# Two changes of order in a two-layer graph network: the second normalisation of a graph stage, and the alternation of bends and gate in the output network

## The chip, the cores and the metric

The kernel runs on one core of a Trainium2 chip. The metric is the device time in microseconds (us) from start to end of one execution. The engines of the core are TensorE (PE, matrix products), VectorE (DVE), ScalarE (ACT, one function per element), GpSimd (POOL) and SyncE (SP, which issues transfers). They run side by side, each in the order of its own program, and wait for each other on semaphores. SBUF is the on-chip memory, PSUM the memory that TensorE writes.

## What is computed

The input x holds 64 graphs of 256 nodes with 256 numbers each; adj holds 64 adjacency matrices of 256 x 256. Four steps follow one another, each on a layer-normalised x and each added to x. The last two are the ones that the change touches:

```python
x = x + _L0_gnn_ref(_layernorm(x), adj, ...)        # gated graph convolution
x = x + _L0_ffn_ref(_layernorm(x), ...)             # an LSTM over the nodes, prefix and suffix sums
x = x + _L1_gnn_ref(_layernorm(x), adj, W, b)       # normalised adjacency times x W, plus b
x = x + _L1_ffn_ref(_layernorm(x), ...)             # the output network, below

t = jnp.max(xx[:, None, :] + Wt[None, :, :], axis=-1) + bt
cvx = jnp.max(z * sl_cvx[None] + of_cvx[None], axis=-1)      # z = t, 8 pieces
ccv = jnp.min(z * sl_ccv[None] + of_ccv[None], axis=-1)
trop = s * cvx + (1.0 - s) * ccv
classical = jax.nn.gelu(xf @ Wc + bc, approximate=False)
g = jax.nn.sigmoid(xf @ Wg + bg)
out = (g * trop + (1.0 - g) * classical) @ Wd + bd
```

## The kernel before

The program is a row of stages with everything in float32: the first graph stage, the LSTM, the second graph stage (`stage_gnn1`), a short stage that turns the 8 + 8 pieces of each of the 1024 hidden units into a base line and a list of hinges, the tropical maximum t (written to DRAM), and the output network (`stage_ffn`).

**The second graph stage** works in rounds of about 10.3 us. In round r five graphs are in work at different lags: `live(0)` is graph r (logits of the LSTM stage and the weighted rows `whf`, `whb`), lag 2 is graph r-2 (x2, its first normalisation `xn`, its degrees), lag 3 is graph r-3 (projection, aggregation, x3 and its statistics), lag 4 is graph r-4 (turned and stored). VectorE's round, in the order of its program: x2 and its statistics (L1006 to L990), `x2b` = x2 + bias (L1011), `xn` (L995, waits for GpSimd's `rstd`), logits and `whf`/`whb` (L1020 to L1028), x3 (L1040, reads TensorE's aggregation), its statistics, two small degree instructions, `s` (L1059), and last the second normalisation `xn3` of the same graph of lag 3 (also L995, since both normalisations go through the helper `normalised`; waits for GpSimd's `rstd3`). A normalisation is two instructions of 128x256. GpSimd takes the variance to the power -0.5: for `rstd` (L817, L819), then adds the identity to the next adjacency (L824), for `rstd3` (L830, L832), then the degrees' power (L838 to L841, `dinv`). TensorE's aggregation (L956) waits for ScalarE's `hs`, and that for `dinv`; the transposes of `xn3` (`ps_xn3t`) and `xn` (`ps_t`), both L906, end TensorE's round. SyncE stores x3 and xn3 of lag 4, then loads `adjt` of lag 1, stores the turned xn3, and loads the next `adj` and `x1`. The rounds 0 to 7 and the last six are written out, the others run in a loop of two rounds.

**The output network** takes tokens in 16 blocks of 1024 and hidden units in 8 groups of 128 per block; one group of one block is called a unit here (u is the group, q = 8m + u the number of the unit in the whole stage, m the block). For a unit, TensorE multiplies x with Wc and Wg in halves of 512 tokens (`products(q, h)`, L2586, into `ps_c` and `ps_g`, one bank each), turns the unit's t into `ps_t` (`turn`, L2578, one buffer), and multiplies the finished unit with Wd (`output_part`, L2599). Its order is: products(q, 0), turn(q+1), products(q, 1), output_part(q-1). ScalarE makes from `ps_t` the base line (L2544) and one rectified hinge per knot: three sure ones (L2549), a number `more[u]` of further ones into the single buffer `spare` (L2556; 5, 2, 2, 1, 1, 1, 1, 1 for the groups 0 to 7), and a last sure one (L2558), which frees `ps_t`. Gelu (L2534, `cls`) and Tanh (L2536, `th`) of the halves lie between. VectorE adds each hinge times its bend onto the line (L2665, 128x1024, each bend depends on the one before), and for the unit before it runs the gate in three instructions, each dependent on the one before: line minus cls (L2645), times (th + 1) (L2648), times 0.5 plus cls into `fused` (L2652). In group 1 `total` (L2661, two instructions) closes the block before: it reads `ps_o`, and TensorE's first output product of a block waits for it.

Before, VectorE's unit is: three bends, (total), the three parts of the gate of the unit before, the fourth bend, the spare bends, and an instruction on one number (`pause`) after which `spare` may be written again.

## Time and profile before

| | us |
|---|---|
| median of 3 runs | 6393.19 (6391.79 to 6393.27) |
| the profiled execution, its own time | 6392.52 |
| its span from first to last instruction | 6390.7 |
| VectorE busy | 5095.3 (80%) |
| TensorE busy | 5520.0 (86%) |
| ScalarE busy | 3238.1 (51%) |
| GpSimd busy | 1914.4 (30%) |

The busy shares are means over stages with different limits, so they do not tell what an edit in one stage is worth. The second graph stage lies at about 1720 to 2390 us, the output network from 4807 us to the end; between them are stages that the change leaves alone. The time of a stage is read from the distance at which one of its instructions comes back, and its limit from the engine that does not wait in that distance. In the rows, "x3" is a run of three instructions, the second number is its length, and the brackets give idle time of the engine just before and what ended it. Instructions of one engine overlap by some hundredths of a microsecond, so a step is measured from start to start.

### The profile page before, as it was taken

How to read it: one execution, taken by the hardware profiler on the slowest of the kernel's cores; microseconds unless marked ns; L12 is line 12 of the kernel's file. 1: busy time of each engine (PE TensorE's matmuls, PEld its weight loads, DVE VectorE, ACT ScalarE, POOL GpSimd, SP SyncE). 2: the span in 40 equal slices, each digit the busy share in tenths (PEclk: the TensorE clock that was granted, in tenths of full speed). 3: DMA queues.
4: the chain of work that ended last, by engine and by line, in shares of the span. 5: the costliest groups of instructions: out<-in, count | busy, mean ns of one | idle time of the engine just before them, and what ended most of it. 6: DMA issues, size and time to landing. Idle time of an engine off the chain costs nothing. (4 is left out here: it accounts for less than half of the span.)

```text
span 6390.7 us, 100252 instructions
## 1 busy us (share of the span) xinstructions
PE 5520.0 (86%) x27318; PEld 3377.2 (53%) x27318; DVE 5095.3 (80%) x9609; ACT 3238.1 (51%) x6025; POOL 1914.4 (30%) x4567
## 2 busy tenths in 40 slices
PE   9998888888788871999999996676667999999999
PEld 6664555555577761666666664444433444444444
DVE  8995444444488877999999998897777999999998
ACT  6663222222244440666666663121116777777777
POOL 3331111111144441555665563147360000000000
PEclk9999999999999995999999998898888999999999
DMA  4441000000144442122212221147352221221221
GB/s 137 134 136 39 0 0 0 0 0 0 41 153 153 153 142 72 69 74 74 73 69 74 74 74 45 54 155 243 109 200 97 79 79 66 86 79 66 79 86 46
DMA packets 359563, 528.72 MB, mean 83 GB/s; under 512 B 28000, under 2 KB 298080, under 8 KB 359424
## 3 DMA queue, kind: packets, MB, share of 16 engines
q1 hardware_dynamic: 323120, 401.16, 19.2%
q0 software_dynamic: 36304, 126.13, 5.8%
q14 instruction: 103, 0.84, 0.0%
q8 instruction: 36, 0.59, 0.0%
HBM read 298.06 MB, written 229.13 MB: 82 GB/s over the span
## 5 line engine op out<-in xcount | busy, mean ns | idle before, releaser
L1743 PE MATMUL t_fetched<-t_wpart,t_onehot 128*128 128x512 f32 x4096 | 1222.3, 420 | 35.6 <-DVE t_tout L1848 15.5
L1848 DVE SCALAR_TENSOR_TENSOR t_tout<-t_fetched,t_top,t_tout 128x1024 f32<-128x1024 f32 x896 | 1149.1, 1282 | 36.4 <-PE t_fetched L1743 5.2
L1743 PEld LDWEIGHTS t_fetched<-t_wpart,t_onehot 128*128 128x128 f32 x4096 | 692.0, 188 | 271.6 <-DVE t_tout L1848 131.4
L2665 DVE SCALAR_TENSOR_TENSOR f_line<-f_hinge,f_vec,f_line 128x1024 f32<-128x1024 f32 x512 | 656.8, 1283 | 60.6 <-ACT f_hinge L2549 45.7
L2171 PE MATMUL ts_fetched<-t_wpart,ts_onehot 128*128 128x512 f32 x1608 | 506.8, 449 | 165.5 <-ACT ts_onehot L2146 66.4
L584 ACT ACTIVATE l_act<-l_ps 128x128 f32<-128x128 f32 x1024 | 228.2, 275 | 716.9 <-PE l_ps L601 716.9
L601 PE MATMUL l_ps<-l_whh,l_ht 128*64 128x256 f32 x4096 | 498.5, 385 | 103.2 <-DVE l_ht L571 103.2
L2599 PE MATMUL f_pso<-f_fused,f_wd 128*128 128x512 f32 x1024 | 464.8, 597 | 36.7 <-DVE f_fused L2652 36.7
L601 PE MATMUL l_ps<-l_wih,l_x 128*64 128x256 f32 x4096 | 485.6, 379 | 1.0 <-DVE l_ps L551 1.0
L2586 PE MATMUL f_psc<-f_x,f_wc 128*128 128x512 f32 x1024 | 485.6, 597 | 0.2
L2586 PE MATMUL f_psg<-f_x,f_wg 128*128 128x512 f32 x1024 | 481.8, 593 | 0.0
L2171 PEld LDWEIGHTS ts_fetched<-t_wpart,ts_onehot 128*128 128x128 f32 x1608 | 304.2, 207 | 316.6 <-DVE ts_tout L2239 209.2
L2143 ACT ACTIVATE ts_dist<-ts_index,t_pminus 128x256 f32<-128x256 f32 (+2 forms) x140 | 79.5, 568 | 656.3 <-PE ts_index L2162 626.1
L601 PEld LDWEIGHTS l_ps<-l_whh,l_ht 128*64 128x64 f32 x4096 | 271.7, 136 | 262.6 <-DVE l_ht L571 151.9
L2549 ACT ACTIVATE f_hinge<-f_pst,f_vec 128x1024 f32<-128x1024 f32 x384 | 398.8, 1114 | 0.0
L2239 DVE SCALAR_TENSOR_TENSOR ts_tout<-ts_fetched,ts_top,ts_tout 128x1024 f32<-128x1024 f32 x296 | 380.0, 1284 | 14.4 <-PE ts_fetched L2171 4.0
L518 POOL TENSOR_TENSOR l_pool_pause<-l_pool_zero 1x1 f32<-1x1 f32 x510 | 93.8, 184 | 972.0 <-DVE l_ht L571 956.1
L601 PEld LDWEIGHTS l_ps<-l_wih,l_x 128*64 128x64 f32 x4096 | 294.7, 137 | 148.9 <-issue 1.8
L2599 PEld LDWEIGHTS f_pso<-f_fused,f_wd 128*128 128x128 f32 x1024 | 192.5, 190 | 293.1 <-issue 266.3
L2556 ACT ACTIVATE f_spare<-f_pst,f_vec 128x1024 f32 x224 | 240.7, 1135 | 167.8 <-DVE f_pause L2690 167.6
L2586 PEld LDWEIGHTS f_psg<-f_x,f_wg 128*128 128x128 f32 x1024 | 195.2, 191 | 246.4 <-issue 246.4
L2665 DVE SCALAR_TENSOR_TENSOR f_line<-f_spare,f_vec,f_line 128x1024 f32<-128x1024 f32 x224 | 287.8, 1285 | 44.2 <-DVE f_line L2665 44.2
(389 smaller groups left out, 10719.4 us busy)
## 6 DMA issues: line engine op xcount, KB each, us to landing
t<-t_tout SPq DMA_DIRECT2D x128, 512.0 KB, 2.7
f_t<-t SPq DMA_DIRECT2D x64, 1024.0 KB, 5.3
g_adj<-in_adj SPq DMA_DIRECT2D x128, 256.0 KB, 3.0
g_adjt<-in_adjt SPq DMA_DIRECT2D x128, 256.0 KB, 2.7
t_x<-x_normalised SPq DMA_DIRECT2D x130, 128.0 KB, 2.4
g_x<-in_x SPq DMA_DIRECT2D x64, 256.0 KB, 2.7
x_kept<-g_x SPq DMA_DIRECT2D x64, 256.0 KB, 2.2
g_x<-x_kept SPq DMA_DIRECT2D x64, 256.0 KB, 2.8
```

Of the source, the lines that this page charges most:

```text
L518: pool.tensor_tensor(pool_pause[:, k:k + 1], pool_zero[:, :], pool_zero[:, :], ALU.add)
L584: act.activation(act_g[q][:, :], ps_g[r % 2][:, q // 2, (q % 2) * P:(q % 2 + 1) * P], ACT.Tanh if q == 0 else ACT.Sigmoid)\
L601: mm = pe.matmul(half(j, c2, p), source[:, k, :], w[:, k, 2 * p:2 * p + 2, c2, :], start=False, stop=last and k == KD - 1, skip_group_chec ...
L1743: mm = pe.matmul(fetched[c % RING][:, h * CH:(h + 1) * CH], one_hot[g][:, c % GRP * P:(c % GRP + 1) * P], w_part[part][:, k, h * CH:(h + 1 ...
L1848: dve.scalar_tensor_tensor(t_out[j][:, :], column[:, :], value, t_out[j][:, :], ALU.add, ALU.max)\
L2171: mm = pe.matmul(fetched[buf][:, h * CH:(h + 1) * CH], one_hot[b][:, at * P:(at + 1) * P], w_part[part][:, half, h * CH:(h + 1) * CH], sta ...
L2239: dve.scalar_tensor_tensor(t_out[j][:, :], column[:, :], top[j][:, c:c + 1], (t_out if c else t_in)[j][:, :], ALU.add, ALU.max).then_inc(f ...
L2549: op = act.activation(hinge[v][:, k, :], ps_t[:, :], ACT.Relu, bias=column(u, "knot", k))
L2556: act.activation(spare[:, ds(k, 1), :].rearrange("p o t -> p (o t)"), ps_t[:, :], ACT.Relu, bias=column(u, "knot", k + SURE))
L2586: mm = pe.matmul(ps_[:, :], w_[:, k, u * P:(u + 1) * P], x[j][:, k, h * HB:(h + 1) * HB], start=(k == 0), stop=(k == KD - 1))
L2599: mm = pe.matmul(ps_o[k][:, h * HB:(h + 1) * HB], w_d[:, u, k * P:(k + 1) * P], fused[u % 2][:, h * HB:(h + 1) * HB], start=(u == 0), stop ...
L2665: dve.scalar_tensor_tensor(acc[:, :], source, column(u, "bend", k), acc[:, :], ALU.mult, ALU.add)\
```

## The change

Two edits of order, neither of which adds or removes arithmetic.

In `stage_gnn1` VectorE's second normalisation moves from the end of the round (graph of lag 3) into the next round (then lag 4), behind `x2b` and ahead of the wait for `rstd`. In `stage_ffn` VectorE takes the gate apart into three pieces and runs one behind each of the first three bends, `total` comes behind them, and ScalarE signals each of the first three hinges by itself and puts Gelu and Tanh of the earlier unit's second half between them.

```diff
@@ stage_gnn1, vector @@
+                if live(4):
+                    n, i, j = graph(4)
+
+                    dve.wait_ge(rstd3_ready, n + 1)
+                    wait_past(dve, x3t_stored[j], 48 * i)
+                    normalised(n, xn3_out[j], x3, mv3, rstd3, xn3_ready)
+                if live(2):
+                    n, i, j = graph(2)
 
                     dve.wait_ge(rstd_ready, n + 1)
                     wait_past(dve, xt_done, n)
...
-                if live(3):
-                    n, i, j = graph(3)
-
-                    dve.wait_ge(rstd3_ready, n + 1)
-                    wait_past(dve, x3t_stored[j], 48 * i)
-                    normalised(n, xn3_out[j], x3, mv3, rstd3, xn3_ready)
@@ stage_ffn, scalar @@
+                    second_half = (lambda u_, q_, h_: None, classical, gate)
                     for k in range(SURE - 1):
-                        op = act.activation(hinge[v][:, k, :], ps_t[:, :], ACT.Relu, bias=column(u, "knot", k))
-                    op.then_inc(sure_ready, 1)
-                    if not (isinstance(q, int) and q == 0):
-                        gate((u - 1) % FT, q - 1, 1)
+                        if not (isinstance(q, int) and q == 0):
+                            second_half[k]((u - 1) % FT, q - 1, 1)
+                        act.activation(hinge[v][:, k, :], ps_t[:, :], ACT.Relu, bias=column(u, "knot", k))\
+                           .then_inc(sure_ready, 1)
...
@@ stage_ffn, vector @@
-                    dve.wait_ge(sure_ready, q + 1)
-                    for k in range(SURE - 1):
+                    for k, fuse_part in enumerate((fuse_diff, fuse_gate, fuse_sum)):
+                        dve.wait_ge(sure_ready, (SURE - 1) * q + k + 1)
                         if k > 0:
                             dve.wait_ge(chain, done + k)
                         bend(u, acc, hinge[v][:, k, :], k)
+                        if not (first and u == 0):
+                            fuse_part((u - 1) % FT, q - 1)
                     if u == 1 and not first:
                         total(m - 1)
-                    if not (first and u == 0):
-                        fuse((u - 1) % FT, q - 1)
```

VectorE at the seam of two rounds of the second graph stage, before (s1 ends the work on one graph, x2 begins the next round; xn30 is the second normalisation's buffer):

```order
L1059 TENSOR_TENSOR g1_s1<-g1_x11,g1_h2 128x512
L995 TENSOR_SCALAR g1_xn30<-g1_x3,g1_mv3,g1_rstd3 128x256 x2
...
L1006 TENSOR_TENSOR g1_x2<-g1_ps_y,g1_s0 128x512
...
L1011 TENSOR_TENSOR g1_x2b0<-g1_x2,g1_b 128x512
L995 TENSOR_SCALAR g1_xn<-g1_x2,g1_mv,g1_rstd 128x256 x2
```

and after:

```order
L1067 TENSOR_TENSOR g1_s1<-g1_x11,g1_h2 128x512
...
L1006 TENSOR_TENSOR g1_x2<-g1_ps_y,g1_s0 128x512
...
L1011 TENSOR_TENSOR g1_x2b0<-g1_x2,g1_b 128x512
L31 ISA
L995 TENSOR_SCALAR g1_xn30<-g1_x3,g1_mv3,g1_rstd3 128x256 x2
L995 TENSOR_SCALAR g1_xn<-g1_x2,g1_mv,g1_rstd 128x256 x2
```

The two instructions of xn30 stand now between x2b0 and xn, four steps later than before.

VectorE in one unit of the output network with one spare bend, before:

```order
L2665 SCALAR_TENSOR_TENSOR f_line3<-f_hinge1,f_vec,f_line3 128x1024
L2677 ISA
L2665 SCALAR_TENSOR_TENSOR f_line3<-f_hinge1,f_vec,f_line3 128x1024
L2677 REGISTER_ALU
L2665 SCALAR_TENSOR_TENSOR f_line3<-f_hinge1,f_vec,f_line3 128x1024
L2645 TENSOR_TENSOR f_line2<-f_line2,f_cls0 128x1024
L2648 SCALAR_TENSOR_TENSOR f_line2<-f_th0,f_line2 128x1024
L2652 SCALAR_TENSOR_TENSOR f_fused0<-f_line2,f_cls0 128x1024
```

and after:

```order
L2681 SCALAR_TENSOR_TENSOR f_line3<-f_hinge1,f_vec,f_line3 128x1024
L2653 TENSOR_TENSOR f_line2<-f_line2,f_cls0 128x1024
L2693 ISA
L2681 SCALAR_TENSOR_TENSOR f_line3<-f_hinge1,f_vec,f_line3 128x1024
L2660 SCALAR_TENSOR_TENSOR f_line2<-f_th0,f_line2 128x1024
L2693 REGISTER_ALU
L2681 SCALAR_TENSOR_TENSOR f_line3<-f_hinge1,f_vec,f_line3 128x1024
L2668 SCALAR_TENSOR_TENSOR f_fused0<-f_line2,f_cls0 128x1024
```

Bends onto line3 and gate parts on line2 alternate, with the same instructions and as many steps of the sequencer. ScalarE in the same place, before:

```order
L2544 ACTIVATE f_line3<-f_pst,f_vec 128x1024
L2549 ACTIVATE f_hinge1<-f_pst,f_vec 128x1024 x3
L2534 ACTIVATE f_cls0<-f_psc,f_vec 128x512
L2536 ACTIVATE f_th0<-f_psg,f_half_bg 128x512
```

and after:

```order
L2549 ACTIVATE f_line3<-f_pst,f_vec 128x1024
L2557 ACTIVATE f_hinge1<-f_pst,f_vec 128x1024
L2535 ACTIVATE f_cls0<-f_psc,f_vec 128x512
L2557 ACTIVATE f_hinge1<-f_pst,f_vec 128x1024
L2541 ACTIVATE f_th0<-f_psg,f_half_bg 128x512
L2557 ACTIVATE f_hinge1<-f_pst,f_vec 128x1024
```

The first hinge comes as before, the third two half-width instructions later.

## Rows read from the trace of the kernel before

**Rows 1.** Stages: length, then busy time (instructions) of PE, PEld, DVE, ACT, POOL; PEclk; DMA share; GB/s.

```profile
1760.00:2370.00 610.00, 545.03 (x3075) 463.99 (x3073) 502.50 (x1606) 287.68 (x647) 270.84 (x537) 1.00 0.49 152
4818.00:6391.00 1573.00, 1461.90 (x4124) 691.03 (x4122) 1440.34 (x1284) 1218.60 (x1381) 0.00 (x0) 0.99 0.22 75
```

**Rows 2.** Timeline of VectorE in one round of the second graph stage.

```profile
2061.59 0.74 DVE L995 TENSOR_SCALAR g_xn<-g_x,g_mv,g_rstd 128x256 f32<-128x256 f32 x2 [0.69 <-POOL g_rstd L832]
2062.24 0.69 DVE L1006 TENSOR_TENSOR g_x<-g_ps_y,g_s 128x512 f32<-128x512 f32 x1
...
2063.91 0.66 DVE L1011 TENSOR_TENSOR g_x2b<-g_x,g_b 128x512 f32<-128x512 f32 x1
2065.44 0.99 DVE L995 TENSOR_SCALAR g_xn<-g_x,g_mv,g_rstd 128x256 f32<-128x256 f32 x2 [0.86 <-POOL g_rstd L819]
...
2072.50 0.68 DVE L1006 TENSOR_TENSOR g_x<-g_ps_y,g_s 128x512 f32<-128x512 f32 x1
```

**Rows 3.** Timeline of GpSimd in the same round.

```profile
2060.30 1.16 POOL L832 TENSOR_TENSOR g_rstd<-g_vare,g_half 128x2 f32<-128x2 f32 x1
...
2064.07 0.56 POOL L817 TENSOR_TENSOR g_vare<-g_mv,g_eps 128x2 f32<-128x2 f32 x1 [1.43 <-DVE g_mv L990]
2064.71 0.69 POOL L819 TENSOR_TENSOR g_rstd<-g_vare,g_half 128x2 f32<-128x2 f32 x1
```

**Rows 4.** GpSimd's `keep`, all of its 64: nanoseconds shortest/median/longest.

```profile
L839 POOL TENSOR_TENSOR g_keep<-g_one,g_is_zero x64: 192/302/308, 1731.9 to 2376.6; 128x2 f32<-128x2 f32 x64
```

**Rows 5.** Timeline of TensorE, the two waits of the following round.

```profile
2073.84 1.99 PE L956 MATMUL g_ps_agg<-g_hs,g_adjt 128*128 128x256 f32 x8 [0.49 <-ACT g_hs L865]
2075.67 0.60 PE L906 MATMUL g_ps_xn3t<-g_ident,g_xn 128*128 128x128 f32 x4
2076.75 0.66 PE L906 MATMUL g_ps_t<-g_ident,g_xn 128*128 128x128 f32 x4 [0.48 <-DVE g_xn L995]
```

**Rows 6.** Output network, timeline of VectorE: unit 4 of a block, then units 0 and 1.

```profile
5463.32 3.92 DVE L2665 SCALAR_TENSOR_TENSOR f_line<-f_hinge,f_vec,f_line 128x1024 f32<-128x1024 f32 x3
5467.16 1.22 DVE L2645 TENSOR_TENSOR f_line<-f_line,f_cls 128x1024 f32<-128x1024 f32 x1
...
5469.67 1.23 DVE L2652 SCALAR_TENSOR_TENSOR f_fused<-f_line,f_cls 128x1024 f32<-128x1024 f32 x1
5470.81 1.28 DVE L2665 SCALAR_TENSOR_TENSOR f_line<-f_hinge,f_vec,f_line 128x1024 f32<-128x1024 f32 x1
...
5473.71 3.93 DVE L2665 SCALAR_TENSOR_TENSOR f_line<-f_hinge,f_vec,f_line 128x1024 f32<-128x1024 f32 x3
...
5506.46 3.93 DVE L2665 SCALAR_TENSOR_TENSOR f_line<-f_hinge,f_vec,f_line 128x1024 f32<-128x1024 f32 x3 [0.88 <-ACT f_hinge L2549]
...
5522.84 3.93 DVE L2665 SCALAR_TENSOR_TENSOR f_line<-f_hinge,f_vec,f_line 128x1024 f32<-128x1024 f32 x3
```

**Rows 7.** Timeline of ScalarE in unit 0: base line, the three hinges, last hinge.

```profile
5502.21 1.21 ACT L2544 ACTIVATE f_line<-f_pst,f_vec 128x1024 f32<-128x1024 f32 x1 [0.27 <-PE f_pst L2578]
5503.31 3.12 ACT L2549 ACTIVATE f_hinge<-f_pst,f_vec 128x1024 f32<-128x1024 f32 x3
...
5512.43 1.19 ACT L2558 ACTIVATE f_hinge<-f_pst,f_vec 128x1024 f32<-128x1024 f32 x1
```

**Rows 8.** Timeline of TensorE: one unit without a wait, unit 0's transposes, a slow output product.

```profile
5471.84 3.60 PE L2599 MATMUL f_pso<-f_fused,f_wd 128*128 128x512 f32 x8
5475.27 1.88 PE L2586 MATMUL f_psc<-f_x,f_wc 128*128 128x512 f32 x4
...
5483.01 3.60 PE L2599 MATMUL f_pso<-f_fused,f_wd 128*128 128x512 f32 x8
...
5501.05 1.04 PE L2578 MATMUL f_pst<-f_ident,f_t 128*128 128x128 f32 x8
...
5825.45 5.37 PE L2599 MATMUL f_pso<-f_fused,f_wd 128*128 128x512 f32 x8 [2.15 <-DVE f_fused L2652]
```

**Rows 9.** The chain that ended last: start, length, what; two turns' marks, first and last block.

```profile
4946.00 2.47 DVE f_ox L2661 x2
...
5460.56 3.70 PE f_pso L2599 x8
...
5556.61 3.70 PE f_pso L2599 x8
...
6301.30 2.47 DVE f_ox L2661 x2
```

More of the change, by code:

```diff
@@ L2528, in _, with classical @@
             more, _ = counts(act)
-            def gate(u, q, h):
+            def classical(u, q, h):
                 v, at = u % 2, slice(h * HB, (h + 1) * HB)
@@ L2534, in gate @@
                 act.activation(cls[v][:, at], ps_c[:, :], ACT.Gelu, bias=vec[:, u, 0:1]).then_inc(cls_ready, 1)
+            def gate(u, q, h):
+                v, at = u % 2, slice(h * HB, (h + 1) * HB)
                 act.wait_ge(g_done, 2 * q + h + 1)
@@ L2561, in body @@
                     wait_past(act, fused_ready, q - 1)
+                    classical(u, q, 0)
                     gate(u, q, 0)
             rounds(act, body)
+            classical(FT - 1, BLOCKS * FT - 1, 1)
             gate(FT - 1, BLOCKS * FT - 1, 1)
@@ L2638, in _, with fuse_diff @@
             more, before = counts(dve)
-            def fuse(u, q):
+            def fuse_diff(u, q):
                 v, acc = u % 2, line[u % 4]
@@ L2645, in fuse, with fuse_gate @@
                 dve.tensor_tensor(acc[:, :], acc[:, :], cls[v][:, :], ALU.subtract).then_inc(diff_ready, 1)
+            def fuse_gate(u, q):
+                v, acc = u % 2, line[u % 4]
                 dve.wait_ge(diff_ready, q + 1)
@@ L2648, in fuse, with fuse_sum @@
                 dve.scalar_tensor_tensor(acc[:, :], th[v][:, :], 1.0, acc[:, :], ALU.add, ALU.mult).then_inc(gated_ready, 1)
+            def fuse_sum(u, q):
+                v, acc = u % 2, line[u % 4]
                 dve.wait_ge(gated_ready, q + 1)
@@ L2692, in _ @@
             rounds(dve, body)
-            fuse(FT - 1, BLOCKS * FT - 1)
+            for fuse_part in (fuse_diff, fuse_gate, fuse_sum):
+                fuse_part(FT - 1, BLOCKS * FT - 1)
             total(BLOCKS - 1)
```

## The prediction, made before the change was run

> **What bounds the kernel now.** I read the stages' windows first [rows 1], then the timelines of each engine in one round or block, then the chain. The second graph stage is VectorE's: in 610 us it is busy for 502.5 and never waits for TensorE in a steady round. One round is 2072.50 - 2062.24 = 10.26 us (10.3 in the next; 10.28 is the mean I use), and in it VectorE stands still twice, both times for GpSimd: 0.69 us ahead of the second normalisation and 0.86 us ahead of the first [rows 2]. So 10.28 - 1.55 = 8.73 us is its own work. The transfers fill 0.49 of the DMA engines at 152 GB/s, and no engine waits for one. TensorE waits 0.49 and 0.48 us in a round [rows 5]; its own work is at most 10.28 - 0.97 = 9.3 us, and about 8.9 when the restarts behind these waits go as well (my estimate is some 0.2 us each).
>
> In the output network two engines are nearly equal. A unit takes TensorE 5483.01 - 5471.84 = 11.17 us when it does not wait [rows 8], so a block of 8 takes 89.4. VectorE needs 5473.71 - 5463.32 = 10.39 us for a unit with one spare bend; unit 0 with five spares takes 5522.84 - 5506.46 = 16.38 [rows 6]; a spare bend is (16.38 - 10.39) / 4 = 1.5, so unit 2 takes 11.9, and unit 1 with total's 2.4 takes 14.3; the sum is 16.4 + 14.3 + 11.9 + 5 x 10.39 = 94.5. The block comes back after 5556.61 - 5460.56 = 96.05 us, and over the 14 periods between first and last mark (6301.30 - 4946.00) / 14 = 96.8 [rows 9]. It is longer than either engine's work because the chain changes hands: VectorE sets the pace in the heavy units 0 to 2, TensorE in 3 to 7. The loop is: output product of unit 2 (5460.56), TensorE without a wait to the transposes of unit 0 (5501.05), ScalarE's line and three hinges (to 5506.43), VectorE without a wait to the gate of unit 2, next output product.
>
> **First edit: the second normalisation.** Removed is the wait of 0.69 us: when the next round comes to it, `rstd3` is over 2 us old. The pair itself takes 0.65 us (2062.24 - 2061.59) wherever it stands; now it stands in the gap between the end of x2b (2063.91 + 0.66 = 2064.57) and xn (2065.44), 0.87 us, of which it fills 0.65 and leaves 0.22 [rows 2]. Undisturbed, the round is 8.73 + 0.22 = 8.95 us. But GpSimd computes `rstd` in just that gap, and it is touchy there. Its power instruction takes 0.69 us alone and 1.16 when it meets VectorE's `s`; the small `vare` takes 0.56 under x2b [rows 3] and ends 0.06 us behind x2b; `keep`, which meets the second normalisation where that stands now, takes 302 ns in the median and 192 at the shortest [rows 4]. So a GpSimd instruction that starts under VectorE's reading waits until this is over. In the new place `rstd` would start at 2064.71, while xn3 runs from about 2064.50 to 2065.24. If it is held until 0.16 us before that end, as `keep` is, it starts at 2065.08, ends at 2065.77, and the round is 0.37 us longer: 9.3. If it is not held, 8.95. I take 9.15, the middle, somewhat to the `keep` row since that is the same pair of instructions. The ends that I keep are 8.73 (the wait vanishes) and 9.5 (held for the whole pair and `dinv` pushed under x2b too).
>
> The Trainium skill ("SBUF — State Buffer", Who interferes with whom) says that VectorE and GpSimd share one pair of ports, held as a lock: a VectorE instruction with two SBUF inputs, or in a two-port mode, blocks a GpSimd instruction that reads SBUF. The rows of `vare` and `rstd3` agree; whether a tensor_scalar of this form takes the pair is what [rows 4] suggest and the page ties to the mode. By the page at its hardest the round would be 9.4 to 9.5.
>
> TensorE's 8.9 to 9.3 lies just at the forecast: it doesn't undo the gain, but it would stop a round from going to 8.73. xn3's consumers have room: TensorE turns it behind the aggregation, which ended at 2075.67, 1.1 us after the new xn3 is done in its round's terms. Nothing else is queued behind the moved instructions on VectorE but xn, which comes at the same time as before. SyncE's wait for `xn3_ready` now holds the adjt load behind it, but that load already waits for the aggregation of the same round, which ends later; the load is used a round later. The wait for the stores of two graphs earlier gets a round more of slack. So: 60 steady rounds x (10.28 - 9.15) = **68 us**, with ends 60 x 0.8 = 48 and 60 x 1.4 = 84.
>
> **Second edit: alternating bends and gate.** VectorE first. From its first bend to the fourth is 5470.81 - 5463.32 = 7.49 us [rows 6]. Behind an instruction on which it depends, a bend comes at 1.32 us (3.92 for three is 2 x 1.32 + 1.28) and a gate part at 1.25; independent ones come at 5467.16 - 5463.32 - 2.64 = 1.20 behind a bend and at 5470.81 - 5469.67 = 1.14 behind a gate part. In the new order all six steps are independent of the one directly before: 3 x 1.20 + 3 x 1.14 = 7.02, 0.47 less. Four of the six steps existed as dependent ones. VectorE's block is then 94.5 - 8 x 0.47 = 90.7 us.
>
> The Trainium skill ("VectorE: DVE Perf Modes", The DRAIN you can't avoid) says the opposite: the next VectorE instruction waits for the pipe to empty anyway, and a semaphore between two costs nothing. The trace of this kernel disagrees by 0.1 us per step, and the rows decide. By the page the 0.47 would be zero.
>
> ScalarE: VectorE's first bend may start after one hinge, not three; that is 2 us earlier (3.12 for three, about 1.0 apart from start to start, [rows 7]). The second needs Gelu of the second half, whose products end 1.72 us behind the transposes while line and hinge keep ScalarE 2.1, so it does not wait; Tanh's products end at 3.45, ScalarE comes there at 3.7. The third hinge is 1.1 us later than before, 5.3 us behind the transposes' end, and VectorE asks for it 4.7 us after its own first bend, which is not before 2.1: covered. Relu, Gelu, Tanh and Identity already take turns: the 11.4 us from line to last hinge in unit 0 hold ten full-width and two half-width instructions at 1.0 and 0.6 us with no room for a change of tables, so the mixing costs nothing.
>
> Now the loops. The old one shrinks by 2.0 (one hinge) and four times 0.47 (VectorE passes through the first four steps of units 0, 1, 2 and 3): 96.05 - 3.9 = 92.2 us. Another becomes the longest, and this is where the gain stops. It goes through the end of unit 0. `total` now stands behind the gate in unit 1, and the block's first output product waits for it. From that product TensorE works without a wait through the transposes of the next unit 0: 6 x 11.17 less one half's products, 3.43 (5475.27 - 5471.84 is the same number of columns) = 63.6. ScalarE starts 1.16 us behind the transposes' start instead of 0.87 (5502.21 - 5501.05), adds 0.3, and needs 5512.43 + 1.19 - 5502.21 = 11.4 us for line, hinges, Gelu, Tanh, five spares and the last hinge, for which VectorE's fourth bend waits. VectorE then runs 16.38 - 7.49 = 8.9 to the end of unit 0, 7.0 to the end of the gate in unit 1, 2.5 for total. Handing over adds 0.2. Sum: 63.6 + 0.3 + 11.4 + 8.9 + 7.0 + 2.5 + 0.2 = 93.9. In unit 3 the transposes wait for ScalarE's spares of unit 2, up to 0.7 more; I take **94.3 us** a block. New waits: VectorE ahead of the fourth bend of unit 0 (some 2 us) and TensorE ahead of the first output product (some 2 us, now on `total`). Against the mean of 96.8: 15 blocks x 2.5 = **37 us**. Bounds: the loop of 92.2 gives 15 x 4.6 = 69; if the old loop keeps the pace for another reason, near 0. The page's rule would cost one 0.47 in this loop, 7 us of the 37.
>
> **Sum.** 68 + 37 = 105 us. The profiled execution took 6392.5 (span 6390.7 and 1.8 around it), the median is 6393.2: 6393.2 - 105 = **6288**.
>
> **The rivals.**
> The lock decides: `rstd` is held for the whole moved pair and the round goes to 9.45. For it: the `keep` row and the page. Then 60 x 0.83 = 50, and 50 + 37 = 87: 6306.
> The blocks do not shorten: TensorE's new wait for `total` and VectorE's for the last hinge of unit 0 eat what the first bend wins. For it: both waits are on the new loop and its sum is only 2.5 us under the old period. 68 + 5 = 73: 6320.
> The graph stage is held by something the timelines do not show, such as 152 GB/s of transfers [rows 1]; 1.57 MB a round in 9.15 us would be 171 GB/s. Against it: no engine in the round waits for a transfer, and VectorE's gaps end with GpSimd. Only the second edit pays: 6356, or nothing at all, 6393, if both fail.
> More than forecast: rounds at 8.8 and blocks at 92.5 give 60 x 1.45 + 15 x 4.3 = 152: 6241.
> Slower: TensorE's clock. Behind close waits one output product took 5.37 us instead of 3.60 [rows 8]: the granted clock had gone to half (1.2 of 2.4 GHz). A unit at half clock costs 11.2 us more. The new order gathers TensorE's waits around units 0 to 2 (about 4 us within 18). To end above 6393 it would have to eat 105 us: from 10 of the 128 units at half clock on; with 12 it is 6393 + 29 = 6422. Against it: the clock is 0.99 over the stage with 6.7 us of waiting a block, and 4.9 would be left.
>
> **How the numbers follow.** Forecast (both pay about as worked out, 6270 to 6300) 0.56; lock 0.14; blocks unchanged 0.11; more 0.08; graph stage held 0.04; nothing 0.03; slower 0.04. The range takes in the forecast, the lock and the blocks' rival, and the lower bounds of both costs in part: 6255 to 6325. 0.2% is 13 us, about what a measurement of this kernel tells from no change. Faster by more: 0.93; within: 0.03; slower: 0.04.
>
> **What would show it.** In the graph stage: the wait on `rstd3` gone, the one on `rstd` between 0.2 and 0.6, a round of 9.0 to 9.3, GpSimd's `rstd` (L819) over 691 ns. Shown wrong by a round over 9.5 or a wait of VectorE on TensorE. In the output network: 7.0 us from first to fourth bend, a wait ahead of the fourth bend in unit 0, TensorE waiting on `total`'s output, and 94.3 us from total to total. Wrong if TensorE waits more than 6 us a block, or the granted clock of the stage is under 0.97.

## The result, and the profile after

| | before | after |
|---|---|---|
| median of 4 runs each, us | 6392.49 | 6286.26 (6284.35 to 6286.68) |
| span of the profiled execution | 6390.7 | 6284.9 |
| VectorE busy | 5095.3 | 5046.8 |
| mean distance of `total` to `total`, 14 blocks | 96.81 | 95.29 |

The changed kernel takes 0.9834 of the time before, 95% interval 0.9816 to 0.9851, which is 106.2 us less; 6288 was predicted. The sum is nearer than its parts: the graph stage gave 83 us where 68 stood, the output network 23 to 26 where 37 stood.

**The graph stage.** VectorE in one round after the change (start, length, instruction, in brackets the idle time before it and its cause), to be held against [rows 2]:

```profile
2063.76 0.68 DVE L1006 TENSOR_TENSOR g_x<-g_ps_y,g_s 128x512 f32<-128x512 f32 x1
...
2065.43 0.66 DVE L1011 TENSOR_TENSOR g_x2b<-g_x,g_b 128x512 f32<-128x512 f32 x1
2066.01 0.73 DVE L995 TENSOR_SCALAR g_xn<-g_x,g_mv,g_rstd 128x256 f32<-128x256 f32 x2
2067.00 1.00 DVE L995 TENSOR_SCALAR g_xn<-g_x,g_mv,g_rstd 128x256 f32<-128x256 f32 x2 [0.25 <-POOL g_rstd L819]
...
2072.70 0.68 DVE L1006 TENSOR_TENSOR g_x<-g_ps_y,g_s 128x512 f32<-128x512 f32 x1
```

The round is 2072.70 - 2063.76 = 8.94 us; the next one is 8.88, and the steady rounds alternate between these two, 8.91 in the mean. The wait on `rstd3` is gone, the second normalisation stands in the gap, and 0.25 us of the gap of 0.87 is left. GpSimd in the same round, and all 64 of its `rstd` and `keep` (ns, shortest/median/longest), against [rows 3, 4]:

```profile
2066.22 0.74 POOL L819 TENSOR_TENSOR g_rstd<-g_vare,g_half 128x2 f32<-128x2 f32 x1
```

```profile
L819 POOL TENSOR_TENSOR g_rstd<-g_vare,g_half x64: 695/738/742, 1727.4 to 2288.2; 128x2 f32<-128x2 f32 x64
```

```profile
L839 POOL TENSOR_TENSOR g_keep<-g_one,g_is_zero x64: 187/190/206, 1732.5 to 2294.5; 128x2 f32<-128x2 f32 x64
```

`rstd` runs under the moved pair and takes 738 ns instead of 691: it was held up by 0.05 us, not by the 0.37 that I had feared. `keep` is back at 190 ns, since the pair has left it. From the first to the last of the 64 x2 instructions it is now 2285.7 - 1724.9 = 560.8 us; before it was 2368.1 - 1724.3 = 643.8. The difference is the 83 us. First after, then before:

```profile
L1006 DVE TENSOR_TENSOR g_x<-g_ps_y,g_s x64: 676/680/693, 1724.9 to 2285.7; 128x512 f32<-128x512 f32 x64
```

```profile
L1006 DVE TENSOR_TENSOR g_x<-g_ps_y,g_s x64: 681/684/693, 1724.3 to 2368.1; 128x512 f32<-128x512 f32 x64
```

The stage has also met another limit. In the same form as [rows 1], the steady rounds after the change:

```profile
1760.00:2280.00 520.00, 517.76 (x3028) 456.66 (x3026) 489.81 (x1576) 285.12 (x640) 263.13 (x528) 1.00 0.57 176
```

TensorE is now busy for 517.76 of 520 us, and in a round of 8.88 us it goes from one instruction to the next without a gap. So what is left of VectorE's wait could give, taken out alone, some 0.03 us a round (an estimate: the mean of 8.91 against 8.88), not 0.25.

**The output network.** VectorE in units 0 and 1 of a block after the change; L2681 are bends (before: L2665), L2653 and L2668 are the first and the last part of the gate, L2677 is `total`:

```profile
5327.66 1.28 DVE L2681 SCALAR_TENSOR_TENSOR f_line<-f_hinge,f_vec,f_line 128x1024 f32<-128x1024 f32 x1 [2.21 <-ACT f_hinge L2564]
...
5336.46 1.28 DVE L2681 SCALAR_TENSOR_TENSOR f_line<-f_hinge,f_vec,f_line 128x1024 f32<-128x1024 f32 x1
5337.66 1.22 DVE L2653 TENSOR_TENSOR f_line<-f_line,f_cls 128x1024 f32<-128x1024 f32 x1
5338.80 1.28 DVE L2681 SCALAR_TENSOR_TENSOR f_line<-f_hinge,f_vec,f_line 128x1024 f32<-128x1024 f32 x1
...
5342.33 1.22 DVE L2668 SCALAR_TENSOR_TENSOR f_fused<-f_line,f_cls 128x1024 f32<-128x1024 f32 x1
5343.46 2.47 DVE L2677 SCALAR_TENSOR_TENSOR f_ox<-f_pso,f_bd,f_x 128x1024 f32<-128x1024 f32 x2
```

From first bend to the end of the six steps is 5343.46 - 5336.46 = 7.00 us (predicted 7.02, before 7.49), 1.20 behind a bend and 1.14 behind a gate part. The first row is the new wait: the fourth bend of unit 0 stands 2.21 us for ScalarE's last hinge. On TensorE, the wait ahead of the transposes of unit 1, which need the last hinge of unit 0, and the new wait on `total`:

```profile
5327.60 1.70 PE L2586 MATMUL f_pst<-f_ident,f_t 128*128 128x128 f32 x8 [3.02 <-ACT f_hinge L2564]
...
5345.98 3.70 PE L2607 MATMUL f_pso<-f_fused,f_wd 128*128 128x512 f32 x8 [1.00 <-DVE f_ox L2677]
```

So far the forecast. What it did not have is in the chain, read at four consecutive `total`s:

```profile
5247.10 2.47 DVE f_ox L2677 x2
5343.46 2.47 DVE f_ox L2677 x2
5438.06 2.47 DVE f_ox L2677 x2
5534.40 2.47 DVE f_ox L2677 x2
```

The blocks are 96.36, 94.60 and 96.34 us long. The ones of 94.60 are the predicted 94.3; every second one is 1.8 longer. ScalarE's timeline shows why, at the first base line of such a block ("issue": it waits for nothing that the profile shows):

```profile
5316.14 1.20 ACT L2549 ACTIVATE f_line<-f_pst,f_vec 128x1024 f32<-128x1024 f32 x1 [2.01 <-issue]
```

This is where the loop over two blocks turns.

And behind `total` the chain does not go through TensorE's first output product, which waits 1.00 us for it, but around it: through VectorE's spare bends of unit 1, after which `spare` is free, ScalarE's spares and last hinge of unit 2, and TensorE's transposes of unit 3.

```profile
5350.48 2.12 ACT L2562 ACTIVATE f_spare<-f_pst,f_vec 128x1024 f32 x2 [3.52 <-DVE f_pause L2706]
```

```profile
5351.24 1.88 PE L2594 MATMUL f_psg<-f_x,f_wg 128*128 128x512 f32 x4
5353.66 1.09 PE L2586 MATMUL f_pst<-f_ident,f_t 128*128 128x128 f32 x8 [0.54 <-ACT f_hinge L2564]
```

### The profile page after: what moved, and what is told of

It reads as the page before. It is cut to its first block and busy times, and to the rows that moved or that the text cites. A ratio compares the mean times of both kernels' runs of the same rounds, so it can differ in the third digit from the quotient of the medians.

```text
span 6284.9 us, 100540 instructions
## 1 busy us (share of the span) xinstructions
PE 5501.3 (88%) x27318; PEld 3383.4 (54%) x27318; DVE 5046.8 (80%) x9609; ACT 3238.0 (52%) x6025; POOL 1908.9 (30%) x4567
## 5 line engine op out<-in xcount | busy, mean ns | idle before, releaser
L2681 DVE SCALAR_TENSOR_TENSOR f_line<-f_hinge,f_vec,f_line 128x1024 f32<-128x1024 f32 x512 | 655.4, 1280 | 89.2 <-ACT f_hinge L2557 49.9
L2557 ACT ACTIVATE f_hinge<-f_pst,f_vec 128x1024 f32<-128x1024 f32 x384 | 430.5, 1122 | 0.0
L2681 DVE SCALAR_TENSOR_TENSOR f_line<-f_spare,f_vec,f_line 128x1024 f32<-128x1024 f32 x224 | 287.8, 1285 | 44.2 <-DVE f_line L2681 44.2
L1692 ACT ACTIVATE t_tout<-t_fetched,t_top 128x1024 f32<-128x1024 f32 x128 | 143.0, 1117 | 322.7 <-PE t_fetched L1744 322.7
```

The source lines that it names most:

```text
L1692: act.activation(t_out[j][:, :], fetched[0][:, :], ACT.Identity, bias=top[j][:, 0, 0:1]).then_inc(first_ready, 1)
L2557: act.activation(hinge[v][:, k, :], ps_t[:, :], ACT.Relu, bias=column(u, "knot", k))\
L2681: dve.scalar_tensor_tensor(acc[:, :], source, column(u, "bend", k), acc[:, :], ALU.mult, ALU.add)\
```

## The experiments

Each is compared with runs of the kernel before on the same chip beside it; these had medians between 6393 and 6408 us. So differences in time are taken within a comparison; where a run is held against the changed kernel, it is their two gains over the kernel before that are compared. Each gain has an interval of about 6 to 11 us to either side, so a difference of some 10 us between two gains stands on the traces, not on the times.

### Each edit alone

The graph stage alone, and the output network alone; the other stage is as before.

> The second graph stage as changed, the output network as before. Theory (the two edits add up, and the changed trace shows the graph stage 83 us shorter): a round of 8.94 us and 83 us less than before, near 6310. Rival (the 68 us of the prediction were right and the output network gave 37): 6325. Rival (the two stages do not add up, since the trace of one execution was compared): anything else.

> The output network as changed, the second graph stage as before. Theory: blocks of 94.6 and 96.4 us in turn, 23 us less than before, near 6370. Rival (37 us as predicted, the rest of the trace's difference being noise): 6356.

Measured: 6324.16 against 6407.14, that is 83.0 us less (ratio 0.9868, 0.9853 to 0.9883), and 6381.53 against 6407.14, 25.6 less (0.9960, 0.9946 to 0.9973). The two edits add up to 108.6, against 106.2 for both at once, the same within the intervals. The graph stage's 68 and the network's 37 of the prediction are both off, in opposite directions; the theory taken from the changed trace holds. With the graph edit alone the 64 x2 span the same stretch as in the changed kernel:

```profile
L1006 DVE TENSOR_TENSOR g_x<-g_ps_y,g_s x64: 675/679/693, 1725.1 to 2285.8; 128x512 f32<-128x512 f32 x64
```

### The second edit taken apart: VectorE's order, ScalarE's order

Both are written against the changed kernel; in both the graph stage is as before.

```diff
 # VectorE's order alone
-                    second_half = (lambda u_, q_, h_: None, classical, gate)
                     for k in range(SURE - 1):
-                        ...
+                        op = act.activation(hinge[v][:, k, :], ps_t[:, :], ACT.Relu, bias=column(u, "knot", k))
+                    op.then_inc(sure_ready, 1)
+                    if not (isinstance(q, int) and q == 0):
+                        classical((u - 1) % FT, q - 1, 1)
+                        gate((u - 1) % FT, q - 1, 1)
 ...
-                        dve.wait_ge(sure_ready, (SURE - 1) * q + k + 1)
+                        if k == 0:
+                            dve.wait_ge(sure_ready, q + 1)
 # ScalarE's order alone
-                    for k, fuse_part in enumerate((fuse_diff, fuse_gate, fuse_sum)):
+                    for k in range(SURE - 1):
 ...
                         bend(u, acc, hinge[v][:, k, :], k)
-                        if not (first and u == 0):
-                            fuse_part((u - 1) % FT, q - 1)
                     if u == 1 and not first:
                         total(m - 1)
+                    if not (first and u == 0):
+                        for fuse_part in (fuse_diff, fuse_gate, fuse_sum):
+                            fuse_part((u - 1) % FT, q - 1)
```

> Output network only: VectorE alternates bends and gate, but ScalarE keeps its old order and signals the three hinges together; graph stage as before. Theory (a step that does not depend on the one before costs 0.1 us less, and the gate's pieces come out earlier): 7.0 us from first to fourth bend, most of the stage's gain, 15 to 20 us less than before. Rival (by the Trainium skill, VectorE: DVE Perf Modes, The DRAIN you can't avoid, the order of dependent steps costs nothing): 7.5 us from first to fourth bend and 0 to 5 us less.

> Output network only: ScalarE signals each hinge and puts Gelu and Tanh between them, VectorE keeps three bends and then the gate; graph stage as before. Theory: the first bend can start up to 2 us earlier where VectorE waits for hinges, but three bends in a row ask for the third hinge 2.6 us later, which comes 1.1 us later than before; 3 to 9 us less than before. Rival (the earlier first hinge is the larger part of the gain): 15 us less or more. Rival (the later third hinge holds VectorE up): no change or slower.

Measured: VectorE's order alone 6384.12, 23.0 us less than before (0.9961, 0.9947 to 0.9974); ScalarE's alone 6401.91, 5.2 less (0.9991, 0.9982 to 1.0), which is not clear of no change. Three consecutive `total`s in the chain of VectorE's order alone:

```profile
5440.82 2.47 DVE f_ox L2676 x2
5535.41 2.47 DVE f_ox L2676 x2
5631.73 2.47 DVE f_ox L2676 x2
```

94.59 and 96.32 us: the same as with the whole edit. So ScalarE's new order adds nothing on top, within what is measured. The likely reason, argued and not tried: the earlier first hinge is on the old loop, which is no longer the longest; in the loop that is, ScalarE makes one line and nine hinges, besides Gelu and Tanh, in either order before the fourth bend of unit 0.

### Every step tied to the one ahead

```diff
+                        if k > 0 and not (first and u == 0):
+                            dve.wait_ge((diff_ready, gated_ready)[k - 1], q)
                         bend(u, acc, hinge[v][:, k, :], k)
                         if not (first and u == 0):
+                            dve.wait_ge(chain, done + k + 1)
                             fuse_part((u - 1) % FT, q - 1)
```

> On top of the changed kernel: the alternating steps stay in their order, but each waits for the one directly ahead of it, as if it depended on it. Theory (a step that waits for the one ahead costs 0.1 us more): 7.7 us from first to fourth bend instead of 7.0, blocks near 96, 18 to 25 us more than the changed kernel, so that the second edit's gain is gone though the order is there. Rival (by the Trainium skill, VectorE: DVE Perf Modes, The DRAIN you can't avoid, a semaphore between two steps costs nothing, and the gain is that the gate comes earlier): 7.0 us and no change against the changed kernel.

Measured: 6347.61 against 6393.46, 45.9 us less than before, a gain 60 smaller than the changed kernel's. It is also 37 us smaller than that of the graph edit alone: tied, the new order is slower than the old one. In one unit, VectorE's first three steps and the seventh:

```profile
5372.65 1.28 DVE L2681 SCALAR_TENSOR_TENSOR f_line<-f_hinge,f_vec,f_line 128x1024 f32<-128x1024 f32 x1
5374.14 1.23 DVE L2653 TENSOR_TENSOR f_line<-f_line,f_cls 128x1024 f32<-128x1024 f32 x1 [0.21 <-DVE f_line L2681]
5375.51 1.28 DVE L2681 SCALAR_TENSOR_TENSOR f_line<-f_hinge,f_vec,f_line 128x1024 f32<-128x1024 f32 x1
...
5380.65 1.28 DVE L2681 SCALAR_TENSOR_TENSOR f_line<-f_hinge,f_vec,f_line 128x1024 f32<-128x1024 f32 x1
```

8.00 us for the six steps, 1.0 more than without the waits; the order and the arithmetic are the same. The direction is the theory's, the size is larger: I expected 7.7 us and 18 to 25 us in all. The chain shows where the rest comes from. Between the end of the first bend (5373.95) and the start of the first gate part stand two instructions of VectorE's sequencer, the waits that this part always had:

```profile
5373.97 0.05 DVEq L2651
5374.08 0.02 DVEq L2652
```

Where two such instructions follow the wait for the step ahead, the next step comes at 1.49 us (5374.14 - 5372.65); where there is one, behind a gate part, at 1.36 or 1.37; where there is none, behind the second and third bend, at 1.32, which is just what dependent bends have in [rows 6]. In the changed kernel the same sequencer instructions run while the engine works and cost nothing. So the wait for the step ahead costs 0.12 us behind a bend, and what the program puts between it and the step comes on top. The Trainium skill ("VectorE: DVE Perf Modes", The DRAIN you can't avoid) found on copies that a semaphore between two steps costs nothing extra; for these instructions that does not hold. The same section adds that an instruction which is not held starts earlier, and that agrees with 1.20 against 1.32.

### The second normalisation behind the first

Against the kernel before; the output network is as before.

```diff
                     normalised(n, xn, x2, mv, rstd, xn_ready)
+                if live(4):
+                    ...
+                    normalised(n, xn3_out[j], x3, mv3, rstd3, xn3_ready)
 ...
-                if live(3):
-                    ...
-                    normalised(n, xn3_out[j], x3, mv3, rstd3, xn3_ready)
```

> Graph stage only (output network as before): the second normalisation moves into the next round, but behind the first normalisation instead of into the gap ahead of it. Theory (the first edit has two halves: 0.70 us a round for the wait on rstd3 that goes, 0.65 us for filling the gap ahead of rstd): the gap is empty again, GpSimd's rstd takes 691 ns, a round is 8.73 + 0.87 = 9.60 us, and the whole is 41 us less than before against 83 in the gap. Rival (the move as such is the gain and the place is nothing): 83 us less. Rival (in the gap, it holds GpSimd up, so elsewhere is as good): between 60 and 83.

Measured: 6348.09 against 6393.46, 45.4 us less (0.9930, 0.9914 to 0.9947). Both normalisations stand in one row, in two consecutive rounds:

```profile
2059.68 1.64 DVE L995 TENSOR_SCALAR g_xn<-g_x,g_mv,g_rstd 128x256 f32<-128x256 f32 x4 [0.86 <-POOL g_rstd L819]
...
2069.15 1.64 DVE L995 TENSOR_SCALAR g_xn<-g_x,g_mv,g_rstd 128x256 f32<-128x256 f32 x4 [0.86 <-POOL g_rstd L819]
```

The gap of 0.86 is there again and the round is 9.47 us (9.60 was expected). So of the 83 us of the first edit some 45 come from no longer asking for `rstd3` too early, and some 38 from filling the gap.

### The bias behind the second normalisation

```diff
-                    wait_past(dve, x3_ready, n - 1)
-                    dve.tensor_tensor(x2b[j][:, :, :], x2[:, :, :], b_all[:, :, :], ALU.add).then_inc(x2b_ready, 1)
                 if live(4):
                     ...
                     normalised(n, xn3_out[j], x3, mv3, rstd3, xn3_ready)
                 if live(2):
                     n, i, j = graph(2)
+
+                    wait_past(dve, x3_ready, n - 1)
+                    dve.tensor_tensor(x2b[j][:, :, :], x2[:, :, :], b_all[:, :, :], ALU.add).then_inc(x2b_ready, 1)
```

> On top of the changed kernel, graph stage: x2b moves behind the second normalisation, so that GpSimd's vare meets a tensor_scalar instead of a tensor_tensor with two SBUF inputs. Theory (the tensor_tensor holds GpSimd up by 0.35 us, the tensor_scalar hardly, 0.05): vare takes 0.2 us instead of 0.55, the last wait of 0.25 us goes, the round falls from 8.94 to TensorE's own work, about 8.87 or VectorE's 8.7; 4 to 14 us less than the changed kernel. Rival (each VectorE instruction on SBUF holds GpSimd alike): vare still 0.5 us, the wait stays, no change.

Measured: 6309.58 against 6407.18, 97.6 us less than before (0.9846, 0.9830 to 0.9862), some 8 less gain than the changed kernel; the stretch of the 64 x2 says the same, 2293.1 - 1723.9 = 569.2 us against 560.8. `vare` did fall, to 272 ns in the median; but `rstd` rose (GpSimd, then VectorE, in two rounds; then all 64 `rstd`, and the 64 x2):

```profile
2060.54 1.34 POOL L819 TENSOR_TENSOR g_rstd<-g_vare,g_half 128x2 f32<-128x2 f32 x1
...
2069.80 0.74 POOL L819 TENSOR_TENSOR g_rstd<-g_vare,g_half 128x2 f32<-128x2 f32 x1
```

```profile
2060.65 0.68 DVE L1019 TENSOR_TENSOR g_x2b<-g_x,g_b 128x512 f32<-128x512 f32 x1
2061.92 1.00 DVE L995 TENSOR_SCALAR g_xn<-g_x,g_mv,g_rstd 128x256 f32<-128x256 f32 x2 [0.58 <-POOL g_rstd L819]
...
2069.91 0.69 DVE L1019 TENSOR_TENSOR g_x2b<-g_x,g_b 128x512 f32<-128x512 f32 x1
```

```profile
L819 POOL TENSOR_TENSOR g_rstd<-g_vare,g_half x64: 693/1340/1343, 1726.4 to 2295.3; 128x2 f32<-128x2 f32 x64
```

```profile
L1006 DVE TENSOR_TENSOR g_x<-g_ps_y,g_s x64: 676/680/692, 1723.9 to 2293.1; 128x512 f32<-128x512 f32 x64
```

In the first of the two rounds `rstd` began just before x2b, while the second of the pair still ran, and ended 0.69 us (its length alone) behind 2061.19, which is 0.14 us before x2b's end: it was held for the whole of x2b. In the next round x2b again starts 0.11 us behind `rstd`, but `rstd` takes 0.74 us and VectorE does not wait. Over the stage 41 of the 64 took 1.34 us and 21 took 0.74, often in turn, and the rounds mostly alternate between 9.20 and 8.72 us; the median of 1340 ns hides the second kind. What decides between the two is not shown; the starts are alike to 0.03 us. The theory had the two prices right (a tensor_tensor from SBUF holds GpSimd for its length, the tensor_scalar pair for some hundredths) and missed who would meet whom: freeing the short `vare` put the long and critical `rstd` beside the tensor_tensor. And there was little to gain, with TensorE busy almost throughout: from the mean of 8.91 us a round to its 8.88. The Trainium skill ("SBUF — State Buffer", Who interferes with whom) names two SBUF inputs on VectorE as what contends with a GpSimd instruction that reads SBUF; the 41 held rounds agree.

### The last hinge ahead of the spares

```diff
+                    act.activation(hinge[v][:, SURE - 1, :], ps_t[:, :], ACT.Relu, ...).then_inc(sure_ready, 1)
                     wait_past(act, chained, q)
                     with act.Fori(0, more[u]) as k:
-                        act.activation(spare[:, ds(k, 1), :]..., ps_t[:, :], ACT.Relu, ...)
-                    act.activation(hinge[v][:, SURE - 1, :], ps_t[:, :], ACT.Relu, ...).then_inc(rest_ready, 1)
+                        act.activation(spare[:, ds(k, 1), :]..., ps_t[:, :], ACT.Relu, ...).then_inc(spared, 1)
+                    act.wait_ge(spared, before[FT] * m + before[u] + more[u])
+                    act.activation(act_pause[:, :], half_bg[0:1, 0:1], ACT.Copy).then_inc(rest_ready, 1)
```

VectorE waits for `sure_ready` ahead of the fourth bend and for `spared` ahead of each spare bend. The instruction on one number, `act_pause`, tells TensorE that `ps_t` is free, as the last hinge did.

> On top of the changed kernel: ScalarE makes the last sure hinge ahead of the spares and signals every spare, VectorE waits for the one that it uses. Theory (the block's pace is the loop through ScalarE's five spares and the last hinge of unit 0, VectorE's fourth bend, total, and TensorE to the next unit 0): the wait of 2.2 us ahead of the fourth bend goes, the block falls to about 92.2 us (94 where the loop turns), 25 to 36 us less than the changed kernel, near 6255. Rival (TensorE's waits for total set the pace for themselves, so the wait of VectorE was slack): at most 5 us less.

Measured: 6241.86 against 6393.46, 151.6 us less than before (0.9764, 0.9748 to 0.9781), a gain 45 larger than the changed kernel's, where 25 to 36 were expected. End of the gate, fourth bend and first spare bend of unit 0, where the changed kernel waits 2.21 us:

```profile
5311.04 1.22 DVE L2672 SCALAR_TENSOR_TENSOR f_fused<-f_line,f_cls 128x1024 f32<-128x1024 f32 x1
5312.18 1.28 DVE L2685 SCALAR_TENSOR_TENSOR f_line<-f_hinge,f_vec,f_line 128x1024 f32<-128x1024 f32 x1
5313.66 1.28 DVE L2685 SCALAR_TENSOR_TENSOR f_line<-f_spare,f_vec,f_line 128x1024 f32<-128x1024 f32 x1 [0.20 <-DVE f_line L2685]
```

No wait, and the chain's `total`s stand 91.92 us apart (93.5 where the loop turns):

```profile
5327.95 2.48 DVE f_ox L2681 x2
5419.87 2.48 DVE f_ox L2681 x2
```

So the changed kernel's pace was set through this wait: taking its 2.2 us out took 2.7 out of the block. The block is now near the 92.2 that the prediction gave for the old loop, shrunk, but it is not the old loop that sets it. Between these two `total`s the chain goes through TensorE to the transposes of unit 0, then through ScalarE's hinges and all five spares of unit 0:

```profile
5401.10 5.18 ACT f_spare L2566 x5
```

Of VectorE's steps in units 0 to 2, which made up the old loop, only those of unit 1 just ahead of `total` are on it. That the two numbers are close says nothing of the old loop.

### The blocks written out

```diff
-            for j in range(2):
-                body(0, j, j)
-            with eng.Fori(1, BLOCKS // 2 - 1) as i:
-                ...
-            for j in range(2):
-                body(BLOCKS // 2 - 1, j, BLOCKS - 2 + j)
+            for m in range(BLOCKS):
+                body(m // 2, m % 2, m)
```

Once on the changed kernel, once on the kernel before. In both, six blocks stood in the program and sixteen stand there now.

> On top of the changed kernel: the 16 blocks of the output network written out, no loop over blocks. Theory (every second block is 1.8 us longer because ScalarE and VectorE stand still for 2 to 3 us where the loop turns): all blocks 94.6 us, 10 to 12 us less than the changed kernel. Rival (the longer block comes from TensorE's clock, which goes to half behind a wait of 3 us there): blocks of 94.6 and 96.4 stay. Rival (four times the code costs fetches of its own): slower, stalls at other places.

> The kernel before with the 16 blocks of the output network written out. Theory (the prediction set a mean of the old blocks that held six turns of the loop, 96.8 us, against a new block without one, 94.3; that is where its 37 us came from): blocks of 96.0 us throughout, 12 us less than before. Then the second edit is worth 96.0 - 94.5 = 1.5 us a block with or without the loop. Rival (the loop costs the old order nothing, its longer blocks have another reason): no change.

Measured: on the changed kernel 6274.85 against 6393.46, 118.6 less than before, a gain 12 larger than the changed one's; on the kernel before 6392.32 against 6407.18, 14.9 less (0.9976, 0.9967 to 0.9986). Consecutive `total`s of the chain, of the changed kernel written out:

```profile
5341.00 2.48 DVE f_ox L2672 x2
5435.42 2.48 DVE f_ox L2672 x2
5529.84 2.48 DVE f_ox L2672 x2
```

and of the kernel before written out:

```profile
5436.12 2.47 DVE f_ox L2656 x2
5531.70 2.47 DVE f_ox L2656 x2
5627.27 2.47 DVE f_ox L2656 x2
```

94.42 and 95.58 us, with no longer ones in turn (in each, one block of the fourteen is longer by 0.8). The longer blocks were the turns of the loop, in the old order (2.2 us) as in the new (1.8), five among the fourteen. The blocks without a turn fell as well, from 96.07 to 95.58 and from 94.60 to 94.42; why is not shown. Between blocks without a turn the second edit is worth 1.2 us here, and 96.07 - 94.60 = 1.5 in the looped form.

### All together

> The changed kernel with all three: last hinge ahead of the spares, blocks written out, x2b behind the second normalisation. Theory (they shorten different loops and add up): blocks of 91.8 us throughout, a round of 8.8 to 8.9, 6225 to 6235, about 55 us less than the changed kernel. Rival (TensorE's own 89.4 us a block and its clock set in before that): 6240.

> The changed kernel with two of the three: last hinge ahead of the spares and blocks written out; x2b stays where the change has it. Theory (moving x2b cost 8 us, since rstd was then held for the whole of it; the two edits of the output network add up): a round of 8.94, rstd near 740 ns, blocks of 91.6 us, 8 us less than with all three and 165 us less than before (ratio 0.974). Rival (the 8 us of the x2b run are noise of the chip): as with all three, ratio 0.976.

Measured: with all three 6252.61 against 6407.18, 154.6 less than before (0.9760, 0.9743 to 0.9776); without the move of x2b 6242.73 against 6408.38, 165.7 less (0.9742, 0.9728 to 0.9755). The `total`s of both stand 91.56 to 91.57 us apart, so the difference is the graph stage's. The stretch of the 64 x2, with all three, then without the move:

```profile
L1006 DVE TENSOR_TENSOR g_x<-g_ps_y,g_s x64: 676/678/692, 1724.1 to 2294.6; 128x512 f32<-128x512 f32 x64
```

```profile
L1006 DVE TENSOR_TENSOR g_x<-g_ps_y,g_s x64: 675/679/692, 1725.0 to 2285.8; 128x512 f32<-128x512 f32 x64
```

570.5 against 560.8 us, 9.7 more with the move. With all three the gain is 48 us larger than the changed kernel's where about 55 were forecast, since x2b's move costs instead of paying. For the last version 165 us were forecast from the runs before it. The last version is some 59 us faster than the changed kernel, each against its own runs of before.

## Why the prediction was right, step by step

- **The graph stage's wait on `rstd3`.** Right, at 0.70 us a round; the run with the normalisation behind the first one shows this half by itself.
- **The gap ahead of `rstd`.** The pair fits into it as worked out. The mis-sized term of the 68 us is GpSimd's hold-up, for which the prediction took 0.2 us of a possible 0.37: it measured 0.05, the wait that remains 0.25, and the round 8.94 and 8.88 in turn, where 9.15 was taken, the undisturbed one put at 8.95 and 9.0 to 9.3 named as the sign. The step that failed in this term is the reading of [rows 4]: from `keep`'s 302 ns under the pair I took it that an instruction is held for the whole pair. It seems to be held only until the one of the two that is running has read, and to get in between them; `keep` met the second of the pair, `rstd` the first. That it slips in between is argued from the starts, not tried.
- **TensorE as the limit.** Right: its own work was put at about 8.9 us a round, and that is where the round ended. The upper end of the 68 us, 84, is 60 x 1.4, which is TensorE's limit; the end of 8.73 us that the text names would have given 93. The measured 83 stands at this end, not in the middle.
- **The number of rounds.** 60 were counted; the stretch of 64 x2 shows 63 distances, 61 of which shortened, by about 1.3 to 1.4 us. That is the small part of the 15 us missing: 60 x (9.15 - 8.91) gives 14 of them.
- **VectorE's steps.** Right to 0.02 us: 7.00 for 7.02. That it is the missing wait on the step ahead, the tied run shows: with the wait back, steps behind a bend come at 1.32 again where nothing else stands between.
- **The new loop, through ScalarE's spares in unit 0, the fourth bend and `total`.** Right: 94.3 predicted, 94.6 measured in a block without a turn of the loop, both named waits are there (2.21 and 1.00 us, for some 2 each), and taking the first out freed it. The 0.3 missing are in unit 3: its transposes start at 5353.66 instead of 5351.24 + 1.72 = 5352.96 (the products of the other units take 1.72 from start to start), 0.7 late, which the prediction had as the most and took at 0.4. By this way around, `total`'s direct wait on TensorE had 0.5 us to spare.
- **The 37 us.** Mis-sized: its 96.8 was the mean over old blocks with turns of the loop in them, and its 94.3 a block without one. Turns cost the new order as well, 1.8 us each, and 95.29 is the mean to be held against 96.81: 1.5 a block, 23 over 15 blocks, 25.6 measured. The row for it was there to be read before: [rows 9] stand 96.05 us apart and the mean 96.8.
- **ScalarE's share of the second edit.** The 2.0 us of the earlier hinge belong to the old loop and bought nothing measurable in the new one, as the prediction's own sum said. No run shows them: ScalarE's order alone gave 5.2 us in all, not clear of nothing. The prediction could have said that ScalarE's half was then not needed at all.
- **The rivals.** The lock did not decide at this place (8.94, not 9.45), but in 41 of 64 rounds it did when x2b was moved. The transfers did not: they rose to 0.57 of the DMA engines in the shorter rounds without a wait on them. TensorE's granted clock went to half for some instructions (the transposes above took 1.70 us instead of 1.04, behind 3.02 us of waiting; the mean from 5327 to 5332 us is 0.66), and the stage's mean stayed 0.99.

Two errors of 15 and some 12 us, in opposite directions, gave a sum within 2 us. That closeness is luck: the mechanisms were right, the two sizes were not.

## What to carry to other kernels

Where two engines take turns in setting the pace, write down each loop that closes over a period, with its parts, and take the longest before and the longest after: by the prediction's sum the old loop fell by 4 us here, while the block fell by 1.5, because another one was right below it, and the wait on that one named the next edit, worth 45 us. An instruction that has to move should go into the gap of another wait, and what runs beside it in the new place has to be checked on the engine that ends that wait; shortening a small instruction there can push the critical one beside a worse neighbour. A median can hide that rounds come in two kinds; look at consecutive ones. Compare like with like: blocks with a turn of the loop against blocks with one.

## What the runs showed of the hardware

- A VectorE step of 128x1024 that waits for the one directly ahead starts 0.11 to 0.12 us later than one that does not: 1.32 against 1.20 behind a bend, 1.25 against 1.14 behind a gate part; with two sequencer instructions between that wait and the step behind a bend it was 1.49, with one behind a gate part 1.36 to 1.37.
- A power instruction of GpSimd on 128x2 numbers takes 0.69 us alone, 0.74 when it starts under a tensor_scalar of 128x256 on VectorE, and, when a tensor_tensor of 128x512 with two SBUF inputs follows 0.11 us behind its start, 1.34 in 41 rounds and 0.74 in 21.
- Where a loop turned, ScalarE stood still 1.99 to 2.24 us in the changed kernel (five turns) and nothing in the profile released it; writing 16 blocks out removed it at no cost that showed elsewhere in the stage (94.42 us in nearly all blocks).
